# Projections, the attention's way out and the hydra passes' first product as three f16 products each; a third place for W1's chunks; orders listed anew

## What is computed

```python
q = (hidden_states @ Wq.T).reshape(b, s, N_HEADS, HEAD_DIM).transpose(0, 2, 1, 3)
scores = jnp.einsum('bhsd,bhtd->bhst', q, k) / jnp.sqrt(jnp.float32(HEAD_DIM))
attn = jax.nn.softmax(scores, axis=-1)
out = jnp.einsum('bhst,bhtd->bhsd', attn, v)
out = out.transpose(0, 2, 1, 3).reshape(b, s, HID)
return out @ Wo.T
...
zxbcdt = u @ in_w.T          # 128 -> 552, in each of the two hydra passes
...
x = _layernorm(x + _L0_attn_ref(x, ...), axis=-1)
x = _layernorm(x + _L0_ffn_ref(x, ...), axis=-1)
x = _layernorm(x + _L1_attn_ref(x, ...), axis=-1)
x = _layernorm(x + _L1_ffn_ref(x, ...), axis=-1)
```

## Time and profile before

| what | us |
|---|---|
| median of 3 runs | 1452.62 (1449.06 to 1453.59) |
| the profiled execution as a whole | 1458.4 |
| its span, first to last instruction | 1456.3 |
| PE busy | 1377.5 |
| DVE busy | 1045.2 |
| ACT busy | 789.0 |
| POOL busy | 721.5 |

### The profile page before, as it was taken

The page is one execution under the profiler, slowest core; times in us unless marked ns, Lnnn a source line. Parts: engine busy times, 40 slices in busy tenths (PEclk is TensorE's granted clock), DMA queues, the critical chain, the costliest instruction groups (busy, mean ns, idle before and its releaser), DMA issues.

```text
span 1456.3 us, 32199 instructions
## 1 busy us (share of the span) xinstructions
PE 1377.5 (95%) x11646; PEld 996.9 (68%) x11646; DVE 1045.2 (72%) x2322; ACT 789.0 (54%) x1737; POOL 721.5 (50%) x915
## 2 busy tenths in 40 slices
PE   6889999999999989999999889999999999999998
PEld 3546776776677668668777666676767767676875
DVE  5886987887886778776876958877686869575121
ACT  3886877777676667777876243433424432421211
POOL 3655655756567577686545434353425343341211
PEclk8779999999999999999999999999999999999999
DMA  8654478578876556785463100451001000100000
GB/s 251 151 125 95 110 152 158 124 140 151 183 135 129 127 138 138 157 163 99 112 142 77 44 1 16 181 185 49 9 1 45 15 1 8 37 16 16 1 15 16
DMA packets 245120, 135.04 MB, mean 93 GB/s; under 512 B 164506, under 2 KB 228226, under 8 KB 244066
## 3 DMA queue, kind: packets, MB, share of 16 engines
q1 hardware_dynamic: 243724, 132.91, 40.0%
q10 hardware_dynamic: 1238, 0.07, 0.1%
HBM read 75.00 MB, written 19.92 MB: 65 GB/s over the span
## 4 chain that ended last, share of the span: by engine, by line
PE 50%; DVE 19%; issue 7%; DMA 7%; POOL 7%; ACT 5%; SPq 4%; DVEq 0%; ACTq 0%; POOLq 0%
PE ps L1906 14%; PE ps L1731 7%; PE ps L1926 6%; PE ps L1803 3%; PE ps L1692 3%; DMA pt<-stp 2%; PE ps L1793 2%; PE ps L1718 2%; PE ps L1746 2%; DVE xraw L1504 2%; PE ps L1856 2%; PE ps L1819 2%; DMA vs<-in_s1u 2%; DVE nmax L1337 2%; DMA vs<-in_s1g 2%
## 5 line engine op out<-in xcount | busy, mean ns | idle before, releaser
L1906 PE MATMUL ps<-x3h,w1gu 128*128 128x256 f16 x1792 | 299.7, 273 | 5.2 <-DVE prod L1574 5.2
L1207 ACT ACTIVATE Pe<-ps,nmax 128x256 f32<-128x256 f32 (+3 forms) x512 | 251.6, 535 | 72.2 <-DVE nmax L1337 58.1
L1337 DVE TENSOR_REDUCE nmax<-ps 128x1 f32<-128x384 f32 (+3 forms) x352 | 220.6, 634 | 41.4 <-PE ps L1796 39.6
L1906 PE MATMUL ps<-x3l,w1gu 128*128 128x256 f16 x896 | 244.4, 273 | 0.0
L1906 PEld LDWEIGHTS ps<-x3h,w1gu 128*128 128x128 f16 x1792 | 175.5, 98 | 31.5 <-DVE prod L1574 8.2
L1332 DVE TENSOR_TENSOR pt<-ps,pt 128x512 f16<-128x512 f32 (+1 forms) x240 | 152.6, 636 | 33.5 <-ACT pt L1193 31.1
L1102 POOL TENSOR_TENSOR int1l<-prod,int1h 128x256 f16<-128x256 f32 x112 | 93.3, 836 | 147.9 <-ACT int1h L1293 147.9
L1193 ACT ACTIVATE pt<-ps 128x512 f16<-128x512 f32 (+1 forms) x240 | 134.9, 562 | 57.0 <-PE ps L1803 55.2
L1793 PE MATMUL ps<-kT,qT 128*128 128x256 f16 (+3 forms) x512 | 139.8, 307 | 9.6 <-ACT Pe L1207 8.6
L1803 PE MATMUL ps<-identf,Pe 128*128 128x128 f32 x880 | 142.0, 282 | 1.3 <-DVE pt L1332 1.2
L1819 PEld LDWEIGHTS ps<-V,pt 128*128 128x128 f16 x2560 | 97.8, 96 | 41.3 <-issue 17.1
(11 more groups left out here) (245 smaller groups left out, 3407.6 us busy)
## 6 DMA issues: line engine op xcount, KB each, us to landing
w1gu<-w_gu SPq DMA_DIRECT2D x7, 1024.0 KB, 8.3
...
w_gu<-vh SPq DMA_DIRECT2D x56, 64.0 KB, 2.2
```

What stands on the lines that cost most here:

```text
L1207: ins = act.activation(Pe[:, u % 2, x * w:(x + 1) * w], ps[:, u % 2, x * w:(x + 1) * w], ACT.Exp, bias=nmax[:, u % 4, x:x + 1])
L1337: dve.tensor_reduce(nmax[:, u % 4, 0:g], ps[:, u % 2, 0:g * w].rearrange("p (g w) -> p g w", g=g), AX, ALU.max, negate=True).then_inc(sem( ...
L1906: ins = pe.matmul(ps[:, bank, piece * H2:piece * H2 + H2], w1gu[:, j // 2, 2 * piece + pw, k, cols], px[:, k, h * H2:h * H2 + H2], start=( ...
```

## The change

- The projections of tiles 2 to 15, the way out of all tiles and the hydra passes' "in" are made of f16 halves: weights (scaled by 64, `WA_SCALE`) and x each as a high and a low half, and three products in place of one f32 product. Tiles 0 and 1 (`NF32`) keep f32. ACT still copies the transposed tile, now into the high half, and DVE makes the low half ("xtl", "atl") ahead of the product. The factor 64 goes out again in existing steps: in the rotary tables, scaled once, in V's column of ones, in the sum of x1, in the scale of ACT's copies.
- The f32 weights are loaded into `stp` and three places of `xr` and halved from there by ACT and DVE ("wq_hi", "wq_lo", four of each; "wo_hi", "wo_lo" likewise, when wqkv's are done and two tiles projected). The loads of x for tiles 4 to 6 and the first "p_hi" wait until those places are read.
- A pass's input is halved by ACT and DVE ("uh", "ul"): from `xmid` for an even q, straight from PSUM for an odd one, for which the copy "h_u" goes.
- W1's chunks get a third place (`NVQ`) and come every four units instead of three. Turned probabilities have five places instead of six. Tile 12 is no longer turned by DMA; the low halves of all DMA-turned units are made by POOL (tiles 3, 6 and 7 are new to it).
- The planner gets a `MARGIN` behind some steps (1.5 us behind pt), other costs and other ranks for FFN0. All orders come out anew. The places on which steps of the prediction rest:

The core of the diff:

```diff
-NPT, NST = 6, 3
-PT_TILES, PT_HEADS = (3, 6, 7, 12, 13, 14, 15), (0, 2)
-LO_POOL = (13, 14, 15)
+NPT, NST = 5, 3
+PT_TILES, PT_HEADS = (3, 6, 7, 13, 14, 15), (0, 2)
+LO_POOL = (3, 6, 7, 12, 13, 14, 15)
...
+NVQ = 3
...
+NF32 = 2
+WA_SCALE = 64.0
...
-            A("SP", "w1c", c, 1500, [("w1_lo", c - 2) if c >= 2 else ("w0_lo", NC0 - 1)], r - 6)
+            A("SP", "w1c", c, 1500, [("w1_lo", c - NVQ) if c >= NVQ else ("w0_lo", NC0 - 1)], r - 6)
...
-            A("SP", "wo_load", t, 4000, [], 10)
+            for k in range(KD):
+                A("ACT", "wq_hi", k, 900, [("wqkv_load", 0)], -11 + 0.1 * k)
+                A("DVE", "wq_lo", k, 960, [("wq_hi", k)], -11 + 0.1 * k)
+            A("SP", "wo_load", t, 4000, [("wq_lo", KD - 1), ("proj", NF32 - 1, PROJ_PIECES - 1)], WO_AT)
+            for k in range(KD):
+                A("ACT", "wo_hi", k, 550, [("wo_load", 0)], WO_AT + 2, chain="wq_hi")
+                A("DVE", "wo_lo", k, 690, [("wo_hi", k)], WO_AT + 2, chain="wq_lo")
...
-        A("ACT", "xte", t, 620, [("xT", t), ("proj", t - 1, PROJ_PIECES - 1) if t else None], r, frees=("xT", t))
-        e = self.pieces("proj", t, PROJ_PIECES, 860, [("xte", t), ("wqkv_load", 0)], r, takes=2)
+        A("ACT", "xte", t, 620, [("xT", t), ("proj", t - 1, PROJ_PIECES - 1) if t else None], r, frees=("xT", t) if t < NF32 else None)
+        if t < NF32:
+            e = self.pieces("proj", t, PROJ_PIECES, 860, [("xte", t), ("wqkv_load", 0)], r, takes=2)
+        else:
+            A("DVE", "xtl", t, 690, [("xte", t)], r, frees=("xT", t))
+            e = self.pieces("proj", t, PROJ_PIECES, 640, [("xtl", t), ("wq_lo", KD - 1)], r, takes=2)
...
-            A("ACT", "p_hi", u, 170 + 0.8 * c, [("exp", u), ("pt", PT_DMA[m - NST]) if m >= NST else None], u)
+            A("ACT", "p_hi", u, 170 + 0.8 * c, [("exp", u), ("pt", PT_DMA[m - NST]) if m >= NST else ("wo_lo", KD - 1)], u)
...
-        A("ACT", "ate", t, 610, [("atr", t), ("wo", t - 1, WO_PIECES - 1) if t else None], r, frees=("atr", t))
-        e = self.pieces("wo", t, WO_PIECES, 860, [("ate", t), ("wo_load", 0)], r)
+        A("ACT", "ate", t, 610, [("atr", t), ("wo", t - 1, WO_PIECES - 1) if t else None], r)
+        A("DVE", "atl", t, 690, [("ate", t)], r, frees=("atr", t))
+        e = self.pieces("wo", t, WO_PIECES, 640, [("atl", t), ("wo_lo", KD - 1)], r)
...
-            A("PE", "in", q, 4300, over + [("h_u", q - 1) if q else None, ("xmid", s), ("x3l", (s - 2, 3)) if s > 1 and p == 0 else None], R5)
+            A("ACT", "uh", q, 600, over + ([("h_out", q - 1)] if p else [("xmid", s), ("in", q - 1) if q else None]), R5)
+            A("DVE", "ul", q, 690, [("uh", q)], R5)
+            A("PE", "in", q, 3200, [("ul", q), ("h_u", q - 1) if q and p == 0 else None, ("x3l", (s - 2, 3)) if s > 1 and p == 0 else None], R5)
...
-            A("DVE", "h_u", q, 700, [("h_out", q)] + ([("up", (s - 1, 3))] if s and p == 0 else []), R5)
+            if p:
+                A("DVE", "h_u", q, 700, [("h_out", q)] + ([("up", (s - 1, 3))] if s else []), R5)
...
+MARGIN = {'pt': 1500, 'w1c': 1500, 'dq': 2500, 'dk': 2500, 'x_load': 2000, 'x1_load': 1500}
...
-CH1_AT = [CH0_AT[-1] + 6 + 3 * c for c in range(NC1)]
+CH1_AT = [CH0_AT[-1] + 6 + 4 * c for c in range(NC1)]
...
-FFN0_AT = [(99, 111), (115, 158), (158, 215), (230, 273), (334, 409), (394, 695), (647, 652), (366, 544)]
+FFN0_AT = [(37, 162), (226, 520), (402, 467), (482, 717), (721, 889), (877, 907), (899, 904), (912, 982)]
...
+        load_a = stp[:, :, :].rearrange("p a n -> p (a n)").bitcast(F32)
+        load_b = xr[:, NI:NI + 3, :].rearrange("p a n -> p (a n)")
+        wq_load = [x[:, k * QKV:k * QKV + QKV] for x in (load_a, load_b) for k in range(2)]
+        wo_load = [load_a[:, k * D:k * D + D] for k in range(3)] + [load_b[:, 0:D]]
...
+                    sp.wait_ge(sem("wa_lo"), KD)
+                    sp.wait_ge(sem("proj"), NF32)
+                    sp.dma_start(load_a.rearrange("p (k n) -> p k n", n=D), A["woT"][0:3 * P].rearrange("(k p) n -> p k n", p=P)).then_inc(sem("ld_wa"), 16)
+                    sp.dma_start(wo_load[3], A["woT"][3 * P:D]).then_inc(sem("ld_wa"), 16)
...
+            if NI <= t < NI + 3:
+                sp.wait_ge(sem("wa_lo"), 2 * KD)
...
-                act.activation(xT[:, :, :].rearrange("p k n -> p (k n)"), ps[:, JOB_BANK["xT", key], :], ACT.Copy).then_inc(sem("xte"), 1)
+                if key < NF32:
+                    act.activation(xT32, ps[:, JOB_BANK["xT", key], :], ACT.Copy, scale=WA_SCALE).then_inc(sem("xte"), 1)
+                else:
+                    act.activation(xT[:, 0, :, :].rearrange("p k n -> p (k n)"), ps[:, JOB_BANK["xT", key], :], ACT.Copy).then_inc(sem("xte"), 1)
+            if kind == "wq_hi":
+                if key == 0:
+                    act.wait_ge(sem("ld_wa"), 32)
+                act.activation(wq[0][:, key, 0:512].rearrange("p (h v c) -> p h v c", v=2, c=HD),
+                               wq_load[key][:, 0:512].rearrange("p (v h c) -> p h v c", v=2, c=HD), ACT.Copy, scale=WA_SCALE)
+                act.activation(wq[0][:, key, 512:QKV], wq_load[key][:, 512:QKV], ACT.Copy, scale=WA_SCALE).then_inc(sem("wa_hi"), 1)
...
+                if kind == "uh":
+                    s, p = divmod(key, 2)
+                    if p:
+                        act.wait_ge(sem("h_out"), key)
+                        act.activation(uhl[:, 0, :], ps[:, 2, :], ACT.Copy).then_inc(sem("uh"), 1)
+                    else:
+                        act.wait_ge(sem("xmid"), s + 1)
+                        if key:
+                            act.wait_ge(sem("h_in"), key)
+                        else:
+                            act.wait_ge(sem("pv"), NUNIT)
+                        act.activation(uhl[:, 0, :], xmid[:, s % 2, :], ACT.Copy).then_inc(sem("uh"), 1)
...
+            if kind == "wq_lo":
+                dve.wait_ge(sem("wa_hi"), t + 1)
+                hi, lo = (wq[h][:, t, 0:512].rearrange("p (h v c) -> p h v c", v=2, c=HD) for h in (0, 1))
+                for v in range(2):
+                    dve.scalar_tensor_tensor(out=lo[:, :, v, :], in0=wq_load[t][:, 256 * v:256 * v + 256].rearrange("p (h c) -> p h c", c=HD),
+                                             scalar=WA_SCALE, in1=hi[:, :, v, :], op0=ALU.mult, op1=ALU.subtract)
+                dve.scalar_tensor_tensor(out=wq[1][:, t, 512:QKV], in0=wq_load[t][:, 512:QKV], scalar=WA_SCALE,
+                                         in1=wq[0][:, t, 512:QKV], op0=ALU.mult, op1=ALU.subtract).then_inc(sem("wa_lo"), 1)
+            if kind == "wo_lo":
+                dve.wait_ge(sem("wa_hi"), KD + t + 1)
+                dve.scalar_tensor_tensor(out=wo[1][:, t, :], in0=wo_load[t], scalar=WA_SCALE, in1=wo[0][:, t, :],
+                                         op0=ALU.mult, op1=ALU.subtract).then_inc(sem("wa_lo"), 1)
+            if kind in ("xtl", "atl"):
+                to, source = (xT, "xT") if kind == "xtl" else (aT, "atr")
+                dve.wait_ge(sem("xte" if kind == "xtl" else "ate"), t + 1)
+                dve.tensor_tensor(to[:, 1, :, :].rearrange("p k n -> p (k n)"), ps[:, JOB_BANK[source, t], :],
+                                  to[:, 0, :, :].rearrange("p k n -> p (k n)"), ALU.subtract).then_inc(sem(kind), 1)
...
+            if kind == "ul":
+                s, p = divmod(q, 2)
+                dve.wait_ge(sem("uh"), q + 1)
+                dve.tensor_tensor(uhl[:, 1, :], ps[:, 2, :] if p else xmid[:, s % 2, :], uhl[:, 0, :], ALU.subtract).then_inc(sem("ul"), 1)
...
+            own.did(dve.tensor_scalar(costab[:, :, :], costab[:, :, :], 1.0 / WA_SCALE, 0.0, ALU.mult, ALU.add))
+            own.link(dve.tensor_scalar(sintab[:, :, :], sintab[:, :, :], 1.0 / WA_SCALE, 0.0, ALU.mult, ALU.add))
...
-            if piece < KD:
-                k = piece
-                pe.matmul(ps[:, bank, :], xT[:, k, :], wqkv[:, k, 0:512].rearrange("p (v h c) -> p h v c", v=2, c=HD), start=(k == 0), stop=(k == KD - 1))
-                return
-            for k in (0, 1) if piece == KD else (2, 3):
-                ins = pe.matmul(ps[:, bank + 1, 0:QKV - 512], xT[:, k, :], wqkv[:, k, 512:QKV], start=(k == 0), stop=(k == KD - 1))
+                    pe.wait_ge(sem("ld_wa"), 32)
+                if t == NF32:
+                    pe.wait_ge(sem("wa_lo"), KD)
+                if t < NF32:
+                    pe.wait_ge(sem("xte"), t + 1)
+                else:
+                    pe.wait_ge(sem("xtl"), t - NF32 + 1)
+            first = piece < KD
+            to = ps[:, bank, :] if first else ps[:, bank + 1, 0:QKV - 512]
+            cols = slice(0, 512) if first else slice(512, QKV)
+            for k in (piece,) if first else (0, 1) if piece == KD else (2, 3):
+                if t < NF32:
+                    w = wq_load[k][:, cols]
+                    w = w.rearrange("p (v h c) -> p h v c", v=2, c=HD) if first else w
```

(12 more changed lines are left out.)

148 lines of the change are left out of this document (78 added, 70 removed).

## The result

| | before | after |
|---|---|---|
| median of 4 runs, us | 1450.84 (1446.26 to 1453.59) | 1410.51 (1409.34 to 1413.44) |
| span of the profiled execution | 1456.3 | 1407.5 |
| PE busy / PE idle | 1377.5 / 78.8 | 1330.7 / 76.8 |

What follows compares the result with a forecast made beforehand. PE's own work was taken to set the pace after 126 us; -37.7 + 1.2 + 4.0 + 5 + 8 - 6.8 = -26.3 us, put onto the 1452.62 us median, gave 1426.3 us, range 1406 to 1447.

Steps and rivals of the forecast that it cites:

- The products: PE's work in projections (-19.9 us), way out (-14.4), hydra's first product (-8.7) and tile 12's transposes (+5.3): -37.7 us.
- rival (1): Attention: other engines hold it and PE's savings there turn into idle time; about 1442 us, chance 0.14.
- the product "in" and the transposes: Hydra passes' first product from f16 halves, -8.7 us; tile 12's 48 transposes on PE instead of DMA, +5.3 us.
- The start: Before the first score: twelve wql steps on DVE stand ahead of the first qk_c, +4.0 us.
- The early giveback: Ahead of 126 us: most of what PE saves is given back, ACT and DVE being nearly full, +5 us (0 to +9).
- POOL's tiles: Tiles 3, 6 and 7: POOL's added low halves lose PE's savings in about half of them, +8 us (0 to +20).
- Waits for pt: PE's wait for DMA-turned probabilities goes through the 1.5 us margin, -6.8 us (0 to -12).
- The passes: Hydra passes: first product -8.7 us, +1.2 given back as the odd passes' chain shortens by only 0.5 us; -7.5 us.
- the two giveback terms: Ahead of 126 us, +5 us of PE's savings given back; in tiles 3, 6 and 7, +8 us lost to POOL's halves.
- (2): Whole kernel: stalls shrink too, with the start covered and POOL's and PE's waits reduced; -45.5 us, 1407 us, chance 0.12.
- (3): Attention: POOL's low halves come late and delay exp and PE; 0.65 us a unit gives about 1465 us, chance 0.09.
- (4): 126.4 to 240.9 us: a less busy PE gets clock 0.8, 27 us longer; 1453 us, no change, chance 0.04.

Runs made afterwards that it cites:

- the kernel with four products: Changed kernel plus a low x low product in the projections of tiles 2 to 15 and every way out, lists kept: 1431.4 us.
- the products only: Products of halves with their splits, everything else as in the kernel before, new lists: 1446.4 us, ratio 0.9966 to the kernel before.
- the nudged kernel before: Kernel before with the planner's cost of PE's transposes of x at 460 ns instead of 440, new lists: 1478.9 us.
- The nudged kernel: Changed kernel with the planner's cost of PE's transposes of x at 460 ns instead of 440, new lists: 1430.5 us.
- The rest without the third place: Kernel before, f32 products kept, with the change's other parts except the third place for W1's chunks, new lists: 1448.9 us, ratio 0.998.

## Why the prediction held, and where its steps did not

The direction and the range held, and the size was short by 14 us. The measured time lies outside the forecast's own band (1415 to 1437 us, chance 0.60). Two groups of terms were wrong, the products by some 12 us and the rest by some 26, with opposite signs: that the error came out as small as it did is luck. So are the signs that were to show the forecast: PE's busy time fell by 46.8 us (30 to 40 forecast), the first hydra product came at 749.7 us (760 to 772), and from there it took 657.8 us (661 to 664), each better than its range.

**The products (-37.7 us).** The price of each was right (24 in 2.89 us; DVE's subtraction 0.685 us, ACT's copy 0.60), and so was PE's work: a fourth product adds 30.2 us of busy time where 32.0 were counted. Wrong was the step "a microsecond of PE work taken out after 126 us is nearly a microsecond of time". For projections and way out it is 20.9 us for 32.0 by the kernel with four products, so some 22 us where the sum had 34.3. I had read PE's 94% as room for nothing else. But DVE at 79% and ACT at 74% of the attention (85 and 76% in tile 3's stretch) are close behind, as rival (1) said; it was right on a third of this term.

**The rest (+11.4 us in the sum: 1.2 + 4.0 + 5 + 8 - 6.8).** The kernel with four products is 20.0 us faster than before. Of that the product "in" and the transposes were to give 3.4 us (-8.7 + 5.3) and the small difference of four products 2.3 (34.3 less 32.0). So some 14 us remain as a gain where the sum had 11.4 us of loss. One by one:
- The start (+4.0): the first score is 3.7 us later (40.7, before 37.0), as counted. DVE's twelve steps with their three neighbours fill 14.95 to 20.17 us, and qk_c begins at 20.17 us, 16.24 before.
- The early giveback (+5): it did not appear in these lists. From the first score to tile 2's first score it took 81.9 us instead of 89.4. PE lost 10.5 us of busy time in the first stretch, about twice what some three tiles' projections and one way out save there by the sum (5.2 us). The rest is about what the groups lose that the change doesn't touch, at a granted clock of 0.83 instead of 0.81. With the products only and other lists the same stretch was 0.8 us longer, so the shorter start is not shown to come from the products. Groups of PE's instructions in that stretch (busy us, mean ns, idle before), before and after:

```profile
L1803 PE MATMUL ps<-identf,Pe 128*128 128x128 f32 x88 | 17.0, 328 | 0.0
```

```profile
L1901 PE MATMUL ps<-identf,Pe 128*128 128x128 f32 x88 | 15.8, 309 | 0.7 <-ACT Pe L1255 0.7
```

- POOL's tiles (+8): failed, in sign too. With lists kept POOL's halves save 2.9 us (0 to 10) against DVE's. POOL was as busy as forecast (51.9 us in tile 3's stretch, with the low halves on POOL), and ACT did wait 23.9 us for it, which I had named as the sign of being wrong. It wasn't one here: exp waited 22 us less for DVE.
- Waits for pt (-6.8): gone as forecast, back at 4.4 us without the margin. Whether the time moved by as much is not known, since the lists moved with it.
- The passes: -11.3 us from the first hydra product to the end, against -7.5. The odd chain is as described, ACT's copy at 809.24 us for 0.60, DVE's half at 809.87 for 0.69, product at 811.0.

**The term that was missing.** Both kernels' times hang on lists that a nudge of 20 ns makes 20 and 29 us worse. The sum took the rows of one list as if the next had the same waits. Nudged against nudged the change is worth 48.4 us, and the products alone 32.6 against the nudged kernel before, close to the 37.8 expected, but 5.1 against before as it is. By new lists the products show anything from 5 to 33 us, depending on the draw, and with lists kept the two places of them show 20.9. One nudge was tried on each kernel, so 48.4 is one draw against another, too. That the measured 40.3 us lie near the sum without the two giveback terms (-39.3) is therefore no proof of the remaining terms.

**The rivals.** The measured 1410.5 us is nearest to (2), 1407 us with a chance of 0.12. Its waits for pt went and POOL's for scales fell, but the start was not covered and the products were not worth their full 37.7 us: it has the number without its mechanism. (3) did not occur: PE was idle for only 22.1 us of the attention, 11.7 of them for exp (126 to 745 us). Its own sum was wrong, though: 0.65 us of delay for each of 96 units is 62 us, so 1489 us, not 1465. (4) occurred only in small: the granted clock in the three parts from 122.6 us on is 1.00, 0.99 and 0.99, with 0.97 in the first stretch of the attention and 0.94 in the first pass, where the kernel before had 0.97:

```profile
749.70:811.00 61.30, 54.49 (x376) 37.48 (x375) 47.75 (x126) 22.44 (x47) 25.95 (x23) 0.94 0.11 38
```

A lower busy share did not always go with a lower clock. The kernel with the products only has PE busy for 41.6 of 47.6 us here, at 1.00:

```profile
256.10:303.70 47.60, 41.63 (x410) 29.95 (x409) 34.96 (x74) 27.67 (x69) 31.56 (x52) 1.00 0.51 116
```

The nudged kernel shows what a long wait does. In the second pass, where PE waited the 11.85 us, the granted clock was 0.91, with PE busy 44.5 of 56.3 us; the changed kernel has 1.00 with 53.5 of 57.3:

```profile
822.20:878.50 56.30, 44.45 (x317) 31.94 (x316) 43.92 (x114) 21.31 (x43) 22.12 (x18) 0.91 0.03 10
```

```profile
811.00:868.30 57.30, 53.53 (x401) 39.48 (x399) 47.17 (x120) 24.79 (x50) 24.82 (x21) 1.00 0.03 10
```

PE in order of time behind that wait, products of 256 columns:

```profile
857.95 0.42 PE L1829 MATMUL ps<-xh,w0gl 128*128 128x256 f16 x1
858.16 0.42 PE L1829 MATMUL ps<-xh,w0gh 128*128 128x256 f16 x1
...
860.36 0.27 PE L1829 MATMUL ps<-xh,w0ul 128*128 128x256 f16 x1
860.47 0.27 PE L1829 MATMUL ps<-xh,w0uh 128*128 128x256 f16 x1
```

They start 0.21 us apart until 860.09 us and 0.11 us apart from 860.25 us on. Twelve products at double the price make some 1.2 us: the wait costs a little more than itself. The Trainium skill (TensorE: Matmul & The Clock Gate, What's actually happening) has it that idle stretches throttle the array; the trace agrees.

**What stays open.** How much of the 14 us is DVE's room, the margin, the third place or a luckier list. Two places in the changed kernel's own lists were not tried, as SP's list is made for three; the margin exists only through the lists. No margin and low halves on DVE cost 12 to 16 us more than the other new lists of the changed kernel, which may be those parts or the draw. The rest without the third place has an attention of 645.2 us in its profiled execution, 15.6 less than the kernel before has, but its passes are 1.5 and its tail 3.9 us longer, and its median is only 2.5 us lower; what of this is the rest and what the new list no run separates. That both original lists are good draws out of many is what seven worse ones suggest; it is not shown how they were found.
